# One block for setup and first attention, and the clearing of the expert rows moved into it

## The reference

```
x                                    # 8 x 256 x 128
# layer 0, attention: 16 heads of 8 columns, causal, with one slope per head
q, k, v = x @ Wq.T, x @ Wk.T, x @ Wv.T
s[h,i,j] = q[h,i] . k[h,j] / sqrt(8) + slope[h] * (j - i)     for j <= i
x = layernorm(x + (softmax(s) @ v) @ Wo.T)
# layer 0, experts; layer 1, a delta rule in chunks of 32 tokens, and experts;
# layer 2, retention and experts; layer 3, a linear recurrence
# layer 3, four rounds of 16 experts: a token is sent to a row of a table by expert,
# and each expert works on the rows of its own part of the table
```

## Time and profile before

| | |
|---|---|
| median of 3 runs | 1625.02 us (1619.47 to 1628.88) |
| the profiled execution | 1635.38 us, its span 1633.7 us |
| mean granted TensorE clock | 0.846 of full speed |
| setup block | from 0 to 14.9 us |
| attention, first product to first `v` | 14.9 to 54.0 us |
| attention, last weighted head | ends at 176.2 us |
| second block of the delta scan | 568.2 to 665.0 us |
| the two clearing transfers | 568.2 to about 690 us |
| PE busy over the span | 1196.6 us (73%) |

### The profile page before, as it was taken

How to read it: one execution, slowest core, us unless ns; L and a number is a source line. 1 busy time by engine, 2 the same in 40 slices (tenths; PEclk the granted TensorE clock), 3 DMA queues, 4 the chain that set the end, 5 groups by cost and what they waited for, 6 DMA issues and landing times. The chain is left out here.

```text
span 1633.7 us, 32566 instructions
## 1 busy us (share of the span) xinstructions
PE 1196.6 (73%) x11088; PEld 843.7 (52%) x11088; DVE 883.3 (54%) x2864; ACT 550.0 (34%) x1180; POOL 275.2 (17%) x395
## 2 busy tenths in 40 slices
PE   8899889998933034416999584999609897979782
PEld 4565556664422034203565341555207897979682
DVE  6454434445076835485456577444595365656323
ACT  3466322222221001312222210332301575757572
POOL 2644100001000000000000001221011443434331
PEclk9899999999976555658999796899857798989896
DMA  1300010050000099700650002332440221212111
GB/s 46 76 3 3 2 30 15 15 204 21 0 1 2 21 354 357 254 0 1 134 119 1 7 2 78 104 98 71 161 155 7 66 52 42 52 42 52 44 43 56
DMA packets 94257, 113.99 MB, mean 70 GB/s; under 512 B 14544, under 2 KB 66855, under 8 KB 93472
## 3 DMA queue, kind: packets, MB, share of 16 engines
q1 hardware_dynamic: 85856, 102.32, 21.0%
q0 software_dynamic: 8272, 10.04, 2.1%
HBM read 61.66 MB, written 53.43 MB: 70 GB/s over the span
## 5 line engine op out<-in xcount | busy, mean ns | idle before, releaser
L1807 PE MATMUL m_psY<-large,m_hT 128*128 x992 | 141.4, 287 | 6.4 <-issue 4.0
L1793 PE MATMUL m_psH<-m_xT,m_up 128*128 128x128 f32 x992 | 140.2, 287 | 0.0
L1807 PEld LDWEIGHTS m_psY<-large,m_hT 128*128 128x128 f32 x992 | 128.7, 193 | 7.3 <-issue 7.3
L1793 PEld LDWEIGHTS m_psH<-m_xT,m_up 128*128 128x128 f32 x992 | 129.8, 203 | 0.0
L1733 POOL DMA_INDIRECT rows<-m_ys,m_slot x93 | 90.5, 974 | 129.4 <-DVE m_slot L2001 114.4
L967 DVE SCALAR_TENSOR_TENSOR m_hid<-m_psU,m_wu,m_sg 128x512 f32<-128x512 f32 x64 | 48.1, 751 | 92.2 <-ACT m_sg L954 92.2
L555 DVE TENSOR_REDUCE at_peaks<-at_ps 128x3 f32<-128x384 f32 x128 | 65.4, 552 | 56.8 <-PE at_ps L380 56.8
L1452 PE MATMUL m_acc<-se_place,se_parts 128*128 128x512 bf16 x384 | 89.9, 385 | 0.0
L1850 ACT ACTIVATE m_up<-large 128x512 f32 x124 | 78.1, 630 | 28.2 <-DVE m_valid L1904 17.0
L511 ACT ACTIVATE at_PT<-at_ps,at_bias 128x384 f32<-128x384 f32 x128 | 67.3, 577 | 55.7 <-PE at_ps L390 55.5
L954 ACT ACTIVATE m_sg<-m_psG,m_wu 128x512 f32<-128x512 f32 x64 | 44.0, 687 | 123.3 <-PE m_psU L916 123.3
(11 more groups left out here) (561 smaller groups left out, 2612.0 us busy)
## 6 DMA issues: line engine op xcount, KB each, us to landing
rows<-blank SPq DMA_DIRECT2D x2, 19584.0 KB
m_xs<-rows SPq DMA_DIRECT2D x124, 76.5 KB
large<-in_L_attn_firs SPq DMA_DIRECT2D x4, 2048.0 KB, 16.6
large<-comb_rows SPq DMA_DIRECT2D x64, 128.0 KB, 5.3
se_wu<-in_L_ffn_up SPq DMA_DIRECT2D x32, 192.0 KB
W2T<-in_L_ffn_down_turned SPq DMA_DIRECT2D x1, 4096.0 KB, 12.5
large<-in_L_ffn_up SPq DMA_DIRECT2D x4, 1024.0 KB, 8.4
large<-in_L_ffn_down SPq DMA_DIRECT2D x16, 256.0 KB, 6.9
```

Of the source, the lines that this page charges most:

```text
L1793: m = nc.tensor.matmul(psH[b][:, c * P:(c + 1) * P], up[b][:, c * P:(c + 1) * P], xT[b][:], start=True, stop=True)
L1807: m = nc.tensor.matmul(psY[b][:, 0:wide], hT[b][:, c * P:(c + 1) * P], k.W2[:, bass.ds(e + c * WIDE, wide)], start=(c == 0), stop=(c == C ...
```

## The change

`setup_stage` and its block are gone. The work of it stands in the attention block, spread over the engines' lists. The tokens are loaded in four transfers, and each part has its own transposes and products (`("X", g)` in `PRODUCTS`). `at_pads` is no longer an input: DVE sets it to zero and copies the two weight matrices into their slots. The zeroing of `VA` is cut to 18 of 32 columns, in four pieces. The fills of `QA` on ACT stand each before the copy of a part of the tokens; the fills of `KA` on DVE stand behind the first key copy. V is multiplied by DVE, in four pieces at `u` = 20, 42, 74 and 106. The 16 transfers of Q stand ahead of the first maxima on SP, and the turn of the first maxima comes 2 heads earlier. The clearing is cut into 16 parts of 128 x 8 x 2448 bytes (2448 KB each), three behind each sending of maxima from b = 2 on (and the last one behind b = 7), and it is gone from the scan. The diff, cut to its core, without the removed code of the setup that only moves:

```diff
-def setup_stage(k, a):
-
-    nc = k.nc
-    slopes = (np.float32(1.0) / np.power(np.float32(256.0), (np.arange(HEADS, dtype=np.float32) + 1) / HEADS)).astype(np.float32)
-    sloped, blank = k.tally("ln_scaled"), k.tally("ln_asked")
-    loaded, made, turned, copied = (k.tally(n) for n in ("loaded", "made", "ln_turned", "ln_copied"))
-    with nc.psum_tensor("ps_setup", [P, 4, 512], F32) as ps, nc.psum_tensor("ps_idle", [P, 512], F32) as idle, \
-            nc.Block() as block:
-        @block.sync
...
-            sp.dma_start(k.X[:], a["L0_attn_x"].rearrange("b (t p) d -> p (b t) d", p=P)).then_inc(loaded.sem, 16)
-            for w, n in ((k.at_wq, "Q"), (k.at_wk, "K"), (k.at_wv, "V"), (k.at_wo, "O")):
-                sp.dma_start(w, a[f"L0_attn_W_{n}"]).then_inc(k.tally("at_w_in").sem, 16)
-            sp.dma_start(k.at_pads, a["L0_attn_pads"]).then_inc(k.tally("at_w_in").sem, 16)
...
-            nc.gpsimd.memset(k.at_VA, 0.0).then_inc(made.sem, 1)
...
-    PRODUCTS = (("q", 0), ("k", 0), ("q", 1), ("k", 1), ("q", 2), ("k", 2), ("q", 3), ("k", 3), ("Q", 1), ("K", 1),
-                ("Q", 2), ("K", 2), ("Q", 3), ("K", 3), ("V", 0), ("V", 1), ("V", 2), ("V", 3))
-    BEFORE = {0: range(0, 4), 4: range(4, 6), 8: range(6, 8), 12: range(8, 10), 16: range(10, 12), 20: range(12, 18)}
-    KEYS = {0: 1, 4: 2, 8: 3}
+    PRODUCTS = (("X", 0), ("q", 0), ("k", 0), ("X", 1), ("Q", 1), ("K", 1), ("X", 2), ("Q", 2), ("K", 2),
+                ("X", 3), ("Q", 3), ("K", 3), ("q", 1), ("k", 1), ("q", 2), ("k", 2), ("q", 3), ("k", 3),
+                ("V", 0), ("V", 1), ("V", 2), ("V", 3))
+    BEFORE = {0: range(0, 6), 2: range(6, 9), 4: range(9, 14), 8: range(14, 16), 12: range(16, 18), 16: range(18, 22)}
+    KEYS = {4: 1, 8: 2, 12: 3}
+    WEIGHTS = {20: 0, 42: 1, 74: 2, 106: 3}
...
+                sp.dma_start(wq, a["L0_attn_W_Q"]).then_inc(w_in.sem, 16)
+                sp.dma_start(wk, a["L0_attn_W_K"]).then_inc(w_in.sem, 16)
+                for g in range(4):
+                    sp.dma_start(k.X[:, 4 * g:4 * g + 4, :],
+                                 a["L0_attn_x"][2 * g:2 * g + 2].rearrange("b (t p) d -> p (b t) d", p=P))\
+                        .then_inc(x_in[g].sem, 16)
+                sp.dma_start(wv, a["L0_attn_W_V"]).then_inc(more_w_in.sem, 16)
+                sp.dma_start(wo, a["L0_attn_W_O"]).then_inc(more_w_in.sem, 16)
...
+                sp.wait_ge(*rows_filled.at(4))
                 sp.wait_ge(*copied(PRODUCTS.index(("Q", 3))))
                 for g in range(GROUPS):
                     for i in range(TILES):
                         rows, head = head_rows(g, i)
                         sp.dma_start(QA[rows, g, 512:N], QT[head, 0:N - 512]).then_inc(more_rows_in[g].sem, 16)
-                    if g == 0:
-                        send_peaks(0)
+                send_peaks(0)
                 send_peaks(1)
                 start_delta_loads(k, a, sp)
                 for b in range(2, BATCH):
                     send_peaks(b)
+                    for part in range(3 * (b - 2), min(3 * (b - 1), CLEARINGS)):
+                        clear_rows(k, sp, part)
...
+                nc.gpsimd.memset(k.ones[:], 1.0).then_inc(made.sem, 1)
+                for g in range(4):
+                    nc.gpsimd.memset(VA[:, 4 * g:4 * g + 4, :, 0:18], 0.0).then_inc(made.sem, 1)
+                pool.wait_ge(*made.at(11))
...
+                pool.wait_ge(*keys_filled.at(4))
                 pool.wait_ge(*copied(PRODUCTS.index(("K", 3))))
                 for g in range(GROUPS):
                     for i in range(TILES):
                         rows, head = head_rows(g, i)
                         nc.gpsimd.dma_start(KA[rows, g, 512:N], KT[head, :]).then_inc(more_keys_in.sem, 16)
-                pool.wait_ge(*cleared.at(2))
-                pool.wait_ge(*v_out.at(8))
-                nc.gpsimd.tensor_tensor(VA[:, :, :, 0:18], VA[:, :, :, 0:18],
-                                        k.at_weight[:].unsqueeze(1).unsqueeze(3).to_broadcast([P, T, HEADS, 18]),
-                                        ALU.mult).then_inc(cleared.sem, 1)
...
-                pe.wait_ge(*w_in.at(80))
+                pe.wait_ge(*made.at(2))
+                pe.wait_ge(*ready.at(1))
+                for i in range(WARMING - 4):
+                    nc.tensor.matmul(psO, k.ident[:], k.blank[:, 0:512], start=True, stop=True)
...
+                    if x == "X":
+                        pe.wait_ge(*x_in[i].at(16))
+                        for t in range(4 * i, 4 * i + 4):
+                            m = nc.tensor.transpose(out[:, t % 4 * P:(t % 4 + 1) * P], k.X[:, t, :], k.ident[:])
...
+                        if x == "Q":
+                            pe.wait_ge(*copied(PRODUCTS.index(("X", i))))
...
-                            pe.wait_ge(*v_out.at(8))
+                            pe.wait_ge(*v_scaled.at(b // 2 + 1))
...
-                        o = psO[32 * i:32 * i + 32, half + kt * P:half + SEQ]
+                        o = psO[32 * i:32 * i + 18, half + kt * P:half + SEQ]
...
-                    if done == HEADS + TILES - LEAD:
+                    if done == HEADS + 2 - LEAD:
...
+                def fill(g):
+                    nc.scalar.activation(QA[:, g, 512:N].rearrange("p (x n) -> p x n", n=512),
+                                         k.blank[:, 0:512].unsqueeze(1).to_broadcast([P, 3, 512]), ACT.Identity,
+                                         bias=k.at_ones[:, 0:1]).then_inc(rows_filled.sem, 1)
+
+                fill(0)
...
+                    if x == "X" and g:
+                        fill(g)
                     act.wait_ge(*projected.at(j + 1))
-                    if x == "q":
+                    if x == "X":
+                        nc.scalar.activation(k.XT[:, g * 512:(g + 1) * 512], p, ACT.Copy).then_inc(q_out.sem, 1)
...
+                nc.vector.memset(k.at_pads[:], 0.0)
...
+                dve.wait_ge(*w_in.at(32))
+                for x, w in ((0, wq), (1, wk)):
+                    m = nc.vector.tensor_copy(
+                        k.at_pads[:, x, :, :].rearrange("p g (i c) -> p (g i) c", c=32)[:, :, 2:2 + HD],
+                        w.rearrange("p (h c) -> p h c", c=HD))
+                m.then_inc(ready.sem, 1)
...
+                def weigh_values(g):
+                    dve.wait_ge(*masked.at(3))
+                    dve.wait_ge(*v_out.at(2 * g + 2))
+                    v = VA[:, 4 * g:4 * g + 4, :, 0:18]
+                    nc.vector.tensor_tensor(v, v, k.at_weight[:].unsqueeze(1).unsqueeze(3).to_broadcast([P, 4, HEADS, 18]),
+                                            ALU.mult).then_inc(v_scaled.sem, 1)
+
                 copy_keys(0)
+                for g in range(GROUPS):
+                    nc.vector.tensor_scalar(KA[:, g, 512:N].rearrange("p (b n) -> p b n", n=SEQ),
+                                            k.at_const[:].unsqueeze(1).to_broadcast([P, BATCH - 2, SEQ]),
+                                            k.at_slope[:, g:g + 1], None, ALU.mult).then_inc(keys_filled.sem, 1)
...
+                    if u in WEIGHTS:
+                        weigh_values(WEIGHTS[u])
...
+CLEARINGS = 16
+
+
+def clear_rows(k, sp, part):
 
     zeroed = k.tally("l3_zeroed")
     share = E3 * N // P // 4
-    for rows in k.rows:
-        sp.dma_start(rows.rearrange("(p s r) w -> p s (r w)", p=P, s=share),
-                      k.blank[:].unsqueeze(1).to_broadcast([P, share, 4 * ROW3])).then_inc(zeroed.sem, 16)
+    each = 2 * share // CLEARINGS
+    rows, at = k.rows[part % 2], part // 2 * each
+    sp.dma_start(rows.rearrange("(p s r) w -> p s (r w)", p=P, s=share)[:, at:at + each, :],
+                 k.blank[:].unsqueeze(1).to_broadcast([P, each, 4 * ROW3])).then_inc(zeroed.sem, 16)
...
-            @block.sync
-            def _(sp):
-                clear_rows(k, sp)
...
```

More of the change, by code:

```diff
@@ L285, in attention_stage @@
         peak_in = [k.tally(f"x_in{5 + i}") for i in range(2)]
+        x_in, more_w_in = [k.tally(f"x_in{i}") for i in range(GROUPS)], k.tally("x_in4")
+        made, ready, keys_filled, rows_filled, v_scaled = (
+            k.tally(n) for n in ("made", "ln_scaled", "ln_rooted", "ln_asked", "exped"))
         ps_cm = nc.psum_tensor("at_ps", [P, 8, 512], F32)
@@ L297, in copied @@
                     return v_out.at(2 * i + 2)
-                return q_out.at(sum(y in "qQK" for y, _ in PRODUCTS[:j + 1]))
+                return q_out.at(sum(y in "XqQK" for y, _ in PRODUCTS[:j + 1]))
             @block.sync
             def _(sp):
+                sp.dma_start(wq, a["L0_attn_W_Q"]).then_inc(w_in.sem, 16)
[6 more added lines that the diff above has]
+                sp.dma_start(wo, a["L0_attn_W_O"]).then_inc(more_w_in.sem, 16)
                 def send_peaks(b):
@@ L568, in attention_stage @@
         project_and_add_stage(k, "at", O, QT, wo)
-        w_in.close(80)
-        masked.close(2)
-        projected.close(18)
-        q_out.close(10)
+        w_in.close(32)
+        masked.close(3)
```

(13 more changed lines are left out.)

143 lines of the change are left out of this document (55 added, 88 removed).

## The result

The changed kernel takes 1630.86 us (median of 6 runs, 1628.44 to 1638.26), the kernel before 1621.88 us in the same comparison (6 runs, 1616.87 to 1628.88): ratio 1.006, 95% interval 1.0035 to 1.0085. Forecast were 1628.7 us and "within 0.5%" as the likeliest case; the measured ratio is just on the slow side of that line. As a difference the change costs 9.0 us, where 3.7 were forecast.

What follows compares the result with a forecast made beforehand. PE sets attention's 15.10 us per sequence, maxima with next to no slack; in the scan, clearing-filled DMA engines stop PE for instructions, 35.5 us. Terms -4.3 - 3.0 + 0.5 + 33.0 + 2.0 + 3.0 - 27.5 = +3.7 on 1625.0: 1628.7 us, range 1606 to 1648.

Steps and rivals of the forecast that it cites:

- Step 1: Start of attention to the first `v`: earlier token work and no wait for first maxima, less new gaps; -4.3 us.
- Step 2: First attention sequence, now 16.80 us: runs at full clock without the pause ahead of it; -3.0 us.
- Step 3: V multiplied on DVE in attention: the first piece pushes four maxima, the other three vanish; +0.5 us (0 to +2).
- Step 4: Clearing in attention: from sequence 3 on, maxima wait behind three parts each in SP's queue; +33.0 us (+30 to +38).
- Step 5: End of the clearing: maxima may use the one DMA engine some 9 us behind; +2 us (up to +9).
- Step 6: Attention: PE's pauses lower the clock, uncovered only behind the last one; +3 us (0 to +5).
- Step 7: Delta scan without the clearing: PE's eight stops, 35.5 us in all, become about 1.0 us each; -27.5 us.
- Rival B: Delta scan: the eight PE stops at new code stay without the clearing; sum +31, 1656 us; chance 5%.
- D: Attention and scan: parts take 6.6 us, scan loses 32 us; sum about -9, 1612 us; chance 7%.
- Rival A: Attention: the maxima are not held up by the clearing parts; sum -34.3, 1590.7 us; chance 13%.

Runs made afterwards that it cites:

- experiment 7: Experiment 5's kernel with V multiplied by GpSimd, in four pieces, instead of VectorE; 1599.00 us, ratio 0.9845.
- experiment 1: The changed kernel with its 16 clearing parts put back into the delta scan's second block, the new start kept; 1625.18 us, ratio 1.002.
- experiment 8: The changed kernel with seven matmuls, results unread, ahead of PE's wait for the maxima of sequence 7; 1628.14 us, ratio 1.0017, executions in two groups.
- experiment 2: The kernel before with only the clearing moved into attention, in the same 16 parts as the change; 1632.80 us, ratio 1.0064.
- experiment 3: The changed kernel with two clearing parts behind each sending of maxima instead of three, six behind the last; 1602.86 us, ratio 0.9874.
- experiment 6: The changed kernel with the 16 clearing parts moved from attention to between SP's loads of the first FFN's experts; 1593.40 us, ratio 0.9817.
- experiment 9: The kernel before with only the clearing moved, 16 parts between SP's loads of the experts as in experiment 6; 1595.62 us, ratio 0.9837.
- experiment 11: The changed kernel with the clearing in the scan in two transfers, as the kernel before has it; 1623.17 us, ratio 1.0005.
- experiment 5: The changed kernel with 1, 1, 2, 2, 2, 2, 2 and 4 clearing parts behind the sendings of sequences 0 to 7; 1599.37 us, ratio 0.9853.
- experiment 4: The changed kernel with the maxima sent from GpSimd's queue, the clearing still on SP; 1637.34 us, ratio 1.0081.
- experiment 10: The changed kernel with the clearing in the scan, 16 parts, in packets of 1224 bytes instead of 2448; one execution, 1672.23 us.

## Why the prediction was right

It named two large terms of opposite sign, and both came, in their places and by the mechanism it gave. That the total came so near is partly luck, twice. Several sizes were off and made up for each other, as the list shows. And the forecast of 1628.7 stood on a median of three runs (1625.02) that was 3.1 us above that of the six in the comparison (1621.88): the total missed by 2.2 us, the difference by 5.3 (9.0 against 3.7).

- **Step 1** (start, -4.3) was too hopeful: -1.5 at the first `v` (52.47 against 53.99), -2.3 at the first exponential. PE turned to the tokens at 7.19 (7.7 was said), its waits for the token copies were 1.92, 1.07 and 1.07 us (4.1 against 4.9), and the wait for the first maxima did go. Not in the sum were three pauses of 0.89 us that follow the products of `q` and `k`, where the next group's code waits for nothing that the profile shows. And it is one execution: in the ten profiles with the new start the first exponential comes at 53.1 to 59.1 us, in the three with the old one at 55.7 to 56.4.

```profile
7.19 0.60 PE L292 MATMUL at_ps<-ident,X 128*128 128x128 f32 x4
8.48 1.99 PE L297 MATMUL at_ps<-XT,at_pads 128*128 128x512 f32 x4 [0.69 <-ACT XT L439]
...
12.82 1.96 PE L301 MATMUL at_ps<-XT,large 128*128 128x512 f32 x4 [1.92 <-ACT XT L439]
...
26.74 0.38 PE L318 MATMUL at_ps<-at_maskb,at_identb 128*128 128x256 bf16 x2 [0.89 <-issue]
```

- **Step 2** (first sequence at full clock, -3.0): 14.1 us instead of 16.8, -2.7. Right in this execution. Five of the ten profiles with the new start have 14.1 us; the others have a slow stretch in this sequence and take 14.9 to 18.0.
- **Step 3** (+0.5): right by experiment 7; PE's wait for VectorE beside its first piece is 0.49 us.
- **Step 4** (+33.0) was right in kind and too large in size: sequence 7 came 27.3 us late against the lead that sequence 1 had (22.35 + 4.94). The clearing ran at 371 to 374 GB/s from 100 to 180 us, and the 15 parts ahead of the last maxima took 102.1 us, not 105.9; the price of 7.06 us was from the scan of the kernel before, where 355 was the mean. (The stage is not the reason: experiment 1 has 365 to 374 with the same parts in the scan.) The rest is the way from SP to PE: I added 5.4 us behind the last part, but SP's issue was done at 179.8 us, with the 15th part still moving, and the first exponential came some 2.5 us behind that part's last packets. Against that, the first part began to move 1.0 us later than counted. The signs came a little smaller than said: sequences 19.9 to 21.1 us apart, not 21 to 22, and waits of PE of 2.4 to 4.9 us, not 3 to 7.
- **Step 5** (the lagging DMA engine, +2): nothing of it can be told apart; with some 2.5 us from the 15th part's last packets to the exponential, 1.6 of them from PE to ACT, it had no room.
- **Step 6** (slow clock behind the last pause, +3) was **mis-sized**: +7.0 until the last copy and +4.7 more until the experts' loads, of which experiment 1 shows 3.3 without a wait for maxima. So the pause cost about 8.4. I had taken one slow stretch as the earlier trace rows show it, some 13 us; this one lasts some 31 us (183 to 214). The profile of experiment 8 shows that its part in attention hangs on the pause.
- **Step 7** (-27.5): from its first copy to the gate block it is 70.3 us instead of 97.6, -27.3. Right. Rival B falls: the longest stop at new code in the first two chunks is 1.81 us.

Steps 4, 5 and 6 erred by -5.7, -2.0 and +5.4 (8.4 less 3), steps 1 to 3 together by +1.9 (a lead of 4.9 us at sequence 1 where their sum is 6.8), step 7 by +0.2, and 3.3 us of the start's lead go in the stages behind attention with or without the clearing, which no step had: +3.1 together, on a sum of +3.7, against +6.9 measured at the gate block. Two figures of the prediction do not follow from its own sums: the bounds of steps 4 and 7 make a range of 1621 to 1638 us, not 1611 to 1648, and D's sum of -9 makes 1616, not 1612. Neither carries the forecast.

Rival A is out by the order of the packets in the change, and by experiments 2 and 3 together: the same parts pass unnoticed when they fit between two sendings, and only then. The Trainium skill ("DMA: Bandwidth & Descriptors", Queues, rings and completion order) has each DMA engine serve one queue in ring order. The maxima of sequence 7, sent from 175.35 on, moved at 181.6, 0.4 us ahead of the first packet of the 16th part, so the trace agrees.

The new start, all of the change but the clearing, is worth nothing that these runs can tell from noise: -2.2 us of median by experiments 6 and 9, +1.1 by 11 against the kernel before, while in the profiles its lead of 4.9 us at the last copy was down to 1.6 at the experts' loads in experiment 1. The windows show the granted clock at 0.50 for a few microseconds at other places in each execution, at the start too, where kernels with the same code differ by up to 5 us (the first maxima leave at 45.73 in experiment 6 and at 50.82 in experiment 5). I read this as a gain that is partly lent: the slow stretch then falls on the next work. No experiment shows that, and why it falls where it does stays open.

## What to carry to other kernels

Bulk transfers that have no due time belong where code is in a loop and loads are large and early, not where a block runs new code and not beside a small transfer on the critical path. A queue of its own for the small transfer is no cure. If they must stand together, queue behind each small transfer only what the engines carry until the next one: two parts of 6.8 us in 15.1 us cost next to nothing, three cost 5 us each time. Count the time that the issue of many descriptors holds the issuing engine, since a block ends with its slowest engine. And when the times of one kernel fall into two groups, as in experiment 8, a single profile explains only the group that it is from.

## What the runs showed of the hardware that was not expected

- A DMA from a queue of its own still waits in busy engines: 6.2 us from issue to landing instead of 1.7 (experiment 4), and PE's instruction packets come 3.4 us further apart (experiment 10's table). That is 42 and 32 packets of 0.107 us. The Trainium skill ("DMA: Bandwidth & Descriptors", Queues, rings and completion order) lets an engine change between queues only after 9 to 17 descriptors as a rule and 64 at most; by its typical figures the wait would be an estimated 1 to 1.8 us, by its ceiling 6.8, and the traces lie between. Experiment 10 speaks against a fixed number of descriptors.
- The Trainium skill ("Runtime: NRT & Kernel Launch", Instruction fetch mechanics) calls the crossing of a 16 KiB block mostly hidden. Here it is hidden only where PE takes long enough over a block: in attention, under full DMA engines, the instruction packets of 16 KB come 6 to 18 us apart and PE shows one stop of 0.64 us; in the new code of the scan they come every 3.9 us without the clearing, with stops of up to 1.81 us, and every 7.3 with it, with stops of up to 5.41.
- SP's issue of one part (1024 packets) takes 0.4 us with idle engines, and each further one more: three parts 5.8 us, four 13.9, six 27.2. I read that as waiting for room. Four maxima transfers take 2.2 us of SP alone, 4.5 behind three parts.
- Half as large packets cost a third of the rate: 250 to 269 GB/s (one execution) against 365 to 374 in experiment 1.
